# Wide attention of a fused transformer kernel: first group's key products placed ahead of its first queries, norm weights loaded ahead of the queries' weight

## The chip, the cores and the metric

The kernel runs on one core of one Trainium2 chip. The metric is the device time of one execution in microseconds (us).

## The reference

One launch computes eight residual layers on x of shape (8, 128, 512) with a context ctx of the same shape, all float32: attention, a block-sparse FFN, attention, a rotated linear layer with LoRA, the attention treated here, an fp8-quantised linear layer, an FFT-based attention, and a gated FFN with 4-bit weights. The layer that the change touches is the fifth:

```python
def _L2_xattn_ref(hidden_states, cross_attention_states, attention_mask, Wq, Wk, Wv, Wo, q_norm_w, k_norm_w):
    H, KVH, HD = (32, 8, 128)
    q = (hidden_states @ Wq.T).reshape(bsz, q_len, H, HD).transpose(0, 2, 1, 3)
    k = (cross_attention_states @ Wk.T).reshape(bsz, kv_len, KVH, HD).transpose(0, 2, 1, 3)
    v = (cross_attention_states @ Wv.T).reshape(bsz, kv_len, KVH, HD).transpose(0, 2, 1, 3)
    q = _rmsnorm(q, q_norm_w)
    k = _rmsnorm(jnp.repeat(k, GROUPS, axis=1), k_norm_w)
    scores = jnp.einsum('bhqd,bhkd->bhqk', q, k) / np.sqrt(HD) + attention_mask
    probs = jax.nn.softmax(scores, axis=-1)
    out = jnp.einsum('bhqk,bhkd->bhqd', probs, v)
    return out.transpose(0, 2, 1, 3).reshape(bsz, q_len, H * HD) @ Wo.T

x = x + _L2_xattn_ref(_layernorm(x), ctx_4096, ctx_4096, mask, Wq, Wk, Wv, Wo, q_norm_w, k_norm_w)
```

## The kernel before

The kernel is a row of stages with a barrier of all engines between two of them. The change lies in one, `wide_attention` (L1385), called once for this layer, with the settings of the class `Wide` (L1329 on). Every matrix is held as two float16 halves, high and low; a product of two matrices is three matmuls (L67 high x high, L68, L69 with a low half), so a query product of one batch is 4 x 3 matmuls of 512 columns and a key or value product is 24 matmuls of 128 columns.

The heads are worked through in 8 groups of four query heads and one key/value head, and each group in 8 batches: 64 steps of attention, numbered s = 0 to 63, and a run-in from s = -10. What each step makes is fixed by tables. Queries are made four steps ahead (`queries_at`): query 0 at s = -4, query 1 at -3, and so on. The key and value products of a group, each for two batches, follow `kv_at` (L1339): keys 0 to 3 at -4, -2, 0, 2 and values 0 to 3 at -1, 1, 3, 5, counted from the group's first step. `w_at` says when a group's weights are split into halves: the keys' weight at -10, the four quarters of the queries' weight at -9 to -6, the values' at -5, the output's four at -4 to -1.

Each engine runs its own program, written out as one loop over the same steps, strictly in program order, and waits on semaphores:

- SyncE loads the first group's weights (`load`, L1542), in between transposes the last rows of x (L1547), then the mask (L1552) and the two norm weights (L1553, L1554); in the steps it issues transposing DMAs of queries (L1562), keys (L1567) and probabilities (L1573), and the next group's weights.
- TensorE, in each step: the scores of step s, the products made at s (`make`), the mix of probabilities and values of s - 3 and the output product of s - 4. A query product needs all four quarters of the queries' weight (`weight_ready("wq", g, H - 1)`), a key product the keys' weight. All products take turns in four PSUM banks.
- ScalarE, in each step: the high half of the heads of s - 4, of value products, the squares of query and key products made at s - 1 (L1726), the high half of those made at s - 2 (L1735), the high halves of the step's weights (L1717), the exponentials (L1758). `squares` waits for the low half of the product two before of its kind, `high_of_rows` until that one's transpose has landed.
- VectorE, in each step: the low half of heads, mask and maximum (L1807, L1810), addition to x (L1826), mean of squares (L1839), low half of the probabilities of s - 1 (L1868), low half of rows made at s - 2 (L1857), the normalising of those made at s - 1 (L1844, for keys also the product with the norm weights, L1848), then the low halves of the step's weights (L1874). The two norm weights are multiplied into one at s = -4 (L1885).
- GpSimd: the root of the mean squares (L1923), the reciprocals, normalised probabilities and their high half (L1931, L1938, L1941).

The order within a step on VectorE is, in short:

```python
for use in rows_here(s):      # made at s - 1
    mean(use)
...
for use in rows_split(s):     # made at s - 2
    low_of_rows(use)
for use in rows_here(s):
    normalise(use)            # waits for the root
for use in weights_at(s):
    low_of_weight(use)
```

Of the kernel before, what the change touches and what calls it, by code (L numbers as in the profile page):

```python
# [8 lines left out]
P = 128  # L9
B = 8  # L10
# [61 lines left out]
class Kernel:  # L72
# [19 lines left out]
    def sem(self, name):  # L92
        self.in_use.append(self.nc.alloc_semaphore(name=name))
        return self.in_use[-1]
# [1234 lines left out]
class Wide:  # L1329


    def __init__(self, name, groups, dim, key_tiles, turn_at, q_ahead):
        self.name, self.groups, self.dim, self.key_tiles = name, groups, dim, key_tiles
        self.normed = name == "a2"
        self.turn_at, self.q_ahead = turn_at, q_ahead
        self.heads = 4
        self.banks = (4, 2, 1, 1)
        if self.normed:
            self.kv_at = {-4: ("k", 0), -2: ("k", 1), 0: ("k", 2), 2: ("k", 3), -1: ("v", 0), 1: ("v", 1), 3: ("v", 2), 5: ("v", 3)}  # L1339
            self.w_at = {-10: [("wk", 0)], -9: [("wq", 0)], -8: [("wq", 1)], -7: [("wq", 2)], -6: [("wq", 3)], -5: [("wv", 0)],  # L1340
                         -4: [("wo", 0)], -3: [("wo", 1)], -2: [("wo", 2)], -1: [("wo", 3)]}
        else:
            self.kv_at = {-4: ("k", 0), -3: ("k", 1), -2: ("v", 0), -1: ("v", 1), 0: ("k", 2), 1: ("k", 3), 2: ("v", 2), 3: ("v", 3)}
            self.w_at = {-9: [("wk", 0)], -8: [("wq", 0)], -7: [("wq", 1)], -6: [("wq", 2)], -5: [("wq", 3)], -4: [("wv", 0)],
                         -3: [("wo", 0)], -2: [("wo", 1)], -1: [("wo", 2)], 0: [("wo", 3)]}
        self.first = min(self.w_at)


W1 = Wide("a1", 4, 96, 2, -5, 5)
# [35 lines left out]
def wide_attention(K, A, wq, wk, wv, wo, mask=None, qw=None, kw=None, quant=None, nxt=None):  # L1385
# [12 lines left out]
    with ExitStack() as c:  # L1398
# [3 lines left out]
        sem = lambda n: K.sem(f"{N}_{n}")  # L1402
# [32 lines left out]
            return [("q", u)] if 0 <= u < TOTAL else []  # L1435

        def kv_made_at(s):
            return [(A.kv_at[s - g * B][0], g, A.kv_at[s - g * B][1]) for g in range(G) if s - g * B in A.kv_at]

        def made_at(s):  # L1440
            return queries_at(s) + kv_made_at(s)
# [28 lines left out]
        if A.normed:  # L1470
            by_row = [u for u in all_made if u[0] != "v"]
            ss_done, mean_done, root_done, row_done, row_hi, row_lo = (
                Steps(sem(n), by_row) for n in ("ss", "mean", "root", "row", "row_hi", "row_lo"))
            q_in, k_in = [sem(f"q_in{i}") for i in range(QT)], [sem(f"k_in{i}") for i in range(4)]
            col_in, col_done = sem("col_in"), sem("col_done")

        def landed(engine, use):

# [51 lines left out]
        with nc.Block() as block:  # L1530
            @block.sync
            def _(sp):
                rows = lambda w: w.rearrange("(k p) n -> p k n", p=P)

                def load(kind, g):
                    if kind == "wo":
                        src = wo[g * H * R:(g + 1) * H * R, :].rearrange("(h r) c -> r h c", r=R)
                    else:
                        w = {"wq": wq, "wk": wk, "wv": wv}[kind]
                        n = H * R if kind == "wq" else R  # L1540
                        src = rows(w)[:, :, g * n:(g + 1) * n]
                    sp.dma_start(nat[kind][:, :, :], src).then_inc(w_in[kind], 16)  # L1542

                for kind in ("wk", "wq"):
                    load(kind, 0)
                sp.wait_ge(last_lo_done, 1)
                sp.dma_start_transpose(K.xn_pair[:, :, :, LAST * P:B * P].rearrange("p a k n -> p (a k) n"),  # L1547
                                       last_hl[:, :, :].rearrange("p a n -> p (a n)")).then_inc(last_in, 16)
                for kind in ("wv", "wo"):
                    load(kind, 0)  # L1550
                if A.normed:
                    sp.dma_start(mk[:, :], mask[0, 0, :, :]).then_inc(col_in, 16)  # L1552
                    sp.dma_start(col[:, 0, :], qw.rearrange("(a d) -> a d", a=1).to_broadcast([P, D])).then_inc(col_in, 16)  # L1553
                    sp.dma_start(col[:, 1, :], kw.rearrange("(a d) -> a d", a=1).to_broadcast([P, D])).then_inc(col_in, 16)  # L1554
                for s in steps:
                    for use in rows_split(s):
                        _, _, _, src, _ = rows_of(use)
                        sp.wait_ge(row_lo.sem, row_lo.count(use))
                        if use[0] == "q":
                            if use[1] >= QT:  # L1560
                                scored(sp, use[1] - QT)
                            sp.dma_start_transpose(q_t[use[1] % QT][:, :, :, :].rearrange("p a h n -> p (a h) n"),  # L1562
                                                   src[:, :, :].rearrange("p a n -> p (a n)")).then_inc(q_in[use[1] % QT], 16)
                        else:
                            if use[1]:
                                scored(sp, s_of(use[1] - 1, 2 * use[2] + 1))
                            sp.dma_start_transpose(k_t[use[2]][:, :, :, :].rearrange("p a h n -> p (a h) n"),  # L1567
                                                   src[:, :, :].rearrange("p a n -> p (a n)")).then_inc(k_in[use[2]], 16)
                    for u in live(s - 1):
                        sp.wait_ge(plo_done.sem, plo_done.count(u))  # L1570
                        if u >= PT:
                            sp.wait_ge(o_bank.filled(u - PT), o_bank.n_filled(u - PT))
                        sp.dma_start_transpose(p_t[u % PT][:, :, :, :, :].rearrange("p a t h n -> p (a t h) n"),  # L1573
                                               p_nat[u % 2][:, :, :].rearrange("p a n -> p (a n)")).then_inc(p_in[u % PT], 16)
                    for use in weights_at(s - 1):
                        kind, g, i = use
                        if use == [u for u in all_weights if u[:2] == (kind, g)][-1] and g + 1 < G:
                            sp.wait_ge(wlo_done[kind].sem, wlo_done[kind].count(use))
                            load(kind, g + 1)
                    if s == LOAD:  # L1580
                        for last in (kv_last("k", G - 1), kv_last("v", G - 1), q_last(G - 1)):
                            sp.wait_ge(ring.filled(last), ring.n_filled(last))
                        quant.load_weight(sp, weight_in)
                        quant.load_context(sp, quant_in)
                sp.wait_ge(quant_in, 32)
# [203 lines left out]
            def _(dve):  # L1789
# [7 lines left out]
                def maxima(s):  # L1797
                    if s >= 2:
                        if A.normed:
                            dve.wait_ge(exp_done.sem, exp_done.count(s - 2))  # L1800
                        else:
                            for t in range(KTL):
                                dve.wait_ge(s_bank.freed((s - 2, t)), s_bank.n_drained((s - 2, t)))
                    for t in range(KTL):
                        dve.wait_ge(s_bank.filled((s, t)), s_bank.n_filled((s, t)))
                        if A.normed:
                            dve.tensor_tensor(masked[s % 2][:, :, :], s_bank[(s, 0)][:, :].rearrange("p (h n) -> p h n", h=H),  # L1807
                                              mk[:, :].unsqueeze(1).to_broadcast([P, H, P]), ALU.add).then_inc(s_bank.freed((s, 0)), 1)
                            dve.wait_ge(s_bank.freed((s, 0)), s_bank.n_drained((s, 0)))
                            m = dve.tensor_reduce(negmax[s % 2][:, :], masked[s % 2][:, :, :], AX.X, ALU.max, negate=True)  # L1810
                        else:
                            m = dve.tensor_reduce(negmax[s % 2][:, 2 * t:2 * t + 2],
                                                  s_bank[(s, t)][:, :].rearrange("p (h n) -> p h n", h=2),
                                                  AX.X, ALU.max, negate=True)
                    m.then_inc(max_done.sem, 1)
# [64 lines left out]
                dve.wait_ge(last_hi_done, 1)  # L1880
                dve.tensor_tensor(last_hl[:, 1, :], last_xn[:, :], last_hl[:, 0, :], ALU.subtract).then_inc(last_lo_done, 1)
                for s in steps:
                    if s == -4:
                        dve.wait_ge(col_in, 48)
                        dve.scalar_tensor_tensor(col[:, 0, :], col[:, 0, :], scale / WS, col[:, 1, :],  # L1885
                                                 ALU.mult, ALU.mult).then_inc(col_done, 1)
                        dve.wait_ge(col_done, 1)
# [1819 lines left out]
```

## Time and profile before

| what | value |
|---|---|
| median of 3 runs | 1568.62 us (1567.54 to 1570.8) |
| the profiled execution | 1571.84 us |
| its span | 1570.0 us |
| TensorE matmul busy | 1394.0 us (89%) |
| VectorE busy | 1089.5 us (69%) |
| ScalarE busy | 733.0 us (47%) |
| GpSimd busy | 728.7 us (46%) |
| mean granted clock of TensorE | 0.953 |
| stage of the change | about 697 to 1207 us of the span |

The span runs from the first to the last instruction of the profiled execution. PE is TensorE, PEld its weight loads, DVE VectorE, ACT ScalarE, POOL GpSimd, SPq the DMA issues of SyncE. A row of a timeline has the start and the duration in us, the line, the operation with output <- inputs, their shapes, and in brackets the idle time before it and what ended it. Matmuls overlap: of a run of them the distance from start to start is the price, not the duration of one. The granted clock is 1.00 at 2.4 GHz and 0.50 at 1.2 GHz.

### The profile page before, as it was taken

How to read it: one execution, taken by the hardware profiler on the slowest of the kernel's cores; microseconds unless marked ns; L12 is line 12 of the kernel's file. 1: busy time of each engine (PE TensorE's matmuls, PEld its weight loads, DVE VectorE, ACT ScalarE, POOL GpSimd, SP SyncE). 2: the span in 40 equal slices, each digit the busy share in tenths (PEclk: the TensorE clock that was granted, in tenths of full speed). 3: DMA queues.
4: the chain of work that ended last, by engine and by line, in shares of the span. 5: the costliest groups of instructions: out<-in, count | busy, mean ns of one | idle time of the engine just before them, and what ended most of it. 6: DMA issues, size and time to landing. Idle time of an engine off the chain costs nothing. (4 is left out here: it accounts for less than half of the span.)

```text
span 1570.0 us, 31373 instructions
## 1 busy us (share of the span) xinstructions
PE 1394.0 (89%) x11348; PEld 833.1 (53%) x11348; DVE 1089.5 (69%) x2159; ACT 733.0 (47%) x2388; POOL 728.7 (46%) x719
## 2 busy tenths in 40 slices
PE   5898699995999999759999999999997767659998
PEld 4775344444777777326555555555553234324444
DVE  7897565536767766757878878778778789956222
ACT  4676363212434432127666666666653356435111
POOL 4787441003434435735666666666655025744000
PEclk9999699997999999879999999999999789979999
DMA  7999571108999998556676665555445201275000
GB/s 183 181 174 169 134 155 39 23 6 172 174 181 194 157 147 145 90 111 161 120 138 111 116 131 116 112 121 100 101 78 111 97 1 38 38 151 105 14 27 28
DMA packets 524169, 174.62 MB, mean 111 GB/s; under 512 B 482560, under 2 KB 507456, under 8 KB 523888
## 3 DMA queue, kind: packets, MB, share of 16 engines
q1 hardware_dynamic: 524016, 172.62, 57.8%
q8 instruction: 92, 1.51, 0.4%
q14 instruction: 61, 0.50, 0.1%
HBM read 53.27 MB, written 2.10 MB: 35 GB/s over the span
## 5 line engine op out<-in xcount | busy, mean ns | idle before, releaser
L1923 POOL TENSOR_TENSOR a_q_ss<-a_q_ss,half 128x4 f32<-128x4 f32 x64 | 89.3, 1396 | 183.5 <-DVE a_k_ss L1839 92.8
L67 PE MATMUL bank<-a_wq_hi,xn_pair 128*128 128x512 f16 (+1 forms) x384 | 139.7, 364 | 19.7 <-DVE a_wq_lo L1874 19.0
L1758 ACT ACTIVATE a_probs<-a_masked,a_negmax 128x128 f32<-128x128 f32 x256 | 99.6, 391 | 95.3 <-DVE a_negmax L1810 95.3
L1285 POOL TENSOR_TENSOR a_p_hl<-a_probs,a_p_hl 128x512 f16<-128x512 f32 x64 | 74.3, 1161 | 143.8 <-DVE a_p_hl L1193 143.8
L69 PE MATMUL bank<-a_wq_hi,xn_pair 128*128 128x512 f16 (+1 forms) x384 | 139.5, 363 | 0.0
L68 PE MATMUL bank<-a_wq_lo,xn_pair 128*128 128x512 f16 (+1 forms) x384 | 139.4, 363 | 0.0
L67 PE MATMUL bank<-a_wo_hi,a_o_hi 128*128 128x512 f16 x256 | 98.0, 383 | 10.3 <-DVE x_state L1826 10.3
L68 PE MATMUL bank<-a_wo_lo,a_o_hi 128*128 128x512 f16 x256 | 98.0, 383 | 0.0
L69 PE MATMUL bank<-a_wo_hi,a_o_lo 128*128 128x512 f16 x256 | 97.8, 382 | 0.0
L1807 DVE TENSOR_TENSOR a_masked<-bank,a_mask 128x512 f32<-128x512 f32 x64 | 44.2, 690 | 70.0 <-PE bank L69 69.9
L1938 POOL TENSOR_TENSOR a_normal<-a_probs,a_recip 128x512 f32<-128x512 f32 x64 | 89.8, 1403 | 5.0
L716 POOL TENSOR_TENSOR a_p_hl<-a_probs,a_p_hl 128x512 f16<-128x512 f32 x64 | 77.8, 1226 | 26.3 <-DVE a_p_hl L627 15.6
L67 PE MATMUL bank<-xn_pair,f_w_t 128*128 128x512 f16 (+1 forms) x176 | 67.9, 386 | 18.8 <-DMA xn_pair<-ctx_lo 15.2
L67 PE MATMUL bank<-a_k_t,a_q_t 128*128 128x128 f16 (+1 forms) x384 | 81.1, 237 | 0.7 <-DMA a_q_t<-a_q_hl 0.7
L489 ACT ACTIVATE a_probs<-bank,a_negmax 128x128 f32<-128x128 f32 x256 | 72.7, 383 | 19.0 <-DVE a_negmax L620 18.7
L69 PE MATMUL bank<-a_k_t,a_q_t 128*128 128x128 f16 (+1 forms) x384 | 81.0, 237 | 0.0
L68 PE MATMUL bank<-a_k_t,a_q_t 128*128 128x128 f16 (+1 forms) x384 | 81.0, 237 | 0.0
L1769 ACT ACTIVATE a_o_hi<-bank 128x512 f16<-128x512 f32 x64 | 38.1, 596 | 86.2 <-PE bank L69 86.1
L1186 DVE TENSOR_REDUCE a_negmax<-bank 128x2 f32<-128x512 f32 x64 | 42.9, 691 | 50.7 <-PE bank L69 50.7
L3531 DVE SCALAR_TENSOR_TENSOR f_h<-bank,f_h 128x512 f32<-128x512 f32 (+1 forms) x22 | 15.2, 690 | 88.4 <-PE bank L69 80.1
L1127 ACT ACTIVATE a_probs<-bank,a_negmax 128x256 f32<-128x256 f32 x128 | 53.4, 472 | 37.8 <-DVE a_negmax L1186 37.8
L1726 ACT ACTIVATE a_qn<-bank 128x128 f32<-128x128 f32 x256 | 67.3, 289 | 3.7 <-PE bank L69 3.7
(441 smaller groups left out, 5016.9 us busy)
## 6 DMA issues: line engine op xcount, KB each, us to landing
a_no<-in_L_xattn_Wo SPq DMA_DIRECT2D x9, 1024.0 KB, 6.0
a_nq<-in_L_xattn_Wq SPq DMA_DIRECT2D x8, 1024.0 KB, 5.9
a_n_wq<-in_L_xattn_Wq SPq DMA_DIRECT2D x4, 768.0 KB, 6.6
a_n_wo<-in_L_xattn_Wo SPq DMA_DIRECT2D x4, 768.0 KB, 6.0
a_nk<-in_L_xattn_Wk SPq DMA_DIRECT2D x9, 256.0 KB, 3.1
a_nv<-in_L_xattn_Wv SPq DMA_DIRECT2D x9, 256.0 KB, 4.0
x_state<-in_x SPq DMA_DIRECT2D x8, 256.0 KB, 4.2
a_ctx<-in_ctx_t SPq DMA_DIRECT2D x8, 256.0 KB, 4.3
```

Of the source, the lines that this page charges most:

```text
L67: pe.matmul(out, lh, rh, start=start, stop=False)
L68: pe.matmul(out, lh, rl, start=False, stop=False)
L69: return pe.matmul(out, ll, rh, start=False, stop=stop)
L489: m = act.activation(probs[t % PS][:, h * P:(h + 1) * P], s_bank[t][:, h * P:(h + 1) * P], ACT.Exp, bias=negmax[t % 4][:, h:h + 1])
L716: pool.tensor_tensor(p_hl[t % PS][:, 1, :], probs[t % PS][:, :], p_hl[t % PS][:, 0, :], ALU.subtract).then_inc(plo_done.sem, 1)
L1127: m = act.activation(probs[u % PROBS][:, n, :], s_bank[(s, t)][:, n * KTL * P:(n + 1) * KTL * P], ACT.Exp, bias=negmax[u % 4][:, n:n + 1])
L1285: pool.tensor_tensor(p_hl[s % PN][:, 1, t, :], probs[unit(s, t) % PROBS][:, :, :].rearrange("p h n -> p (h n)"), p_hl[s % PN][:, 0, t, :], ...
L1726: m = act.activation(dst[:, h, :], src[:, h, :], ACT.Square, scale=1.0 / WS, accum_out=sums[:, h:h + 1])
L1758: m = act.activation(probs[s % 2][:, h, :], src, ACT.Exp, bias=negmax[s % 2][:, h:h + 1], accum_out=total[s % 2][:, h:h + 1])
L1807: dve.tensor_tensor(masked[s % 2][:, :, :], s_bank[(s, 0)][:, :].rearrange("p (h n) -> p h n", h=H), mk[:, :].unsqueeze(1).to_broadcast([P ...
L1923: pool.tensor_tensor(r[:, :], r[:, :], K.half[:, 0:n], ALU.pow).then_inc(root_done.sem, 1)
L1938: m = pool.tensor_tensor(normal[s % 2][:, t, :, :], probs[s % 2][:, :, t * P:(t + 1) * P], by, ALU.mult)
```

## The change

The key products of group 0 alone are made at s = -9 to -6, one a step, in place of -4, -2, 0 and 2; those of the other groups stay. The two norm weights are loaded behind the keys' weight and ahead of the queries', with a semaphore of their own, and the mask, still behind the output's weight, has another, on which VectorE waits ahead of its first use. The product of the two norm weights moves from s = -4 to s = -8.

```diff
--- before.py
+++ after.py
@@ -1344,6 +1344,10 @@
             self.w_at = {-9: [("wk", 0)], -8: [("wq", 0)], -7: [("wq", 1)], -6: [("wq", 2)], -5: [("wq", 3)], -4: [("wv", 0)],
                          -3: [("wo", 0)], -2: [("wo", 1)], -1: [("wo", 2)], 0: [("wo", 3)]}
         self.first = min(self.w_at)
+        self.first_kv_at = {**self.kv_at, **dict(zip(range(self.first + 1, self.first + 5), [("k", i) for i in range(4)]))} if self.normed else self.kv_at
+        if self.normed:
+            for s in (-4, -2, 0, 2):
+                del self.first_kv_at[s]
 
 
 W1 = Wide("a1", 4, 96, 2, -5, 5)
@@ -1435,7 +1439,8 @@
             return [("q", u)] if 0 <= u < TOTAL else []
 
         def kv_made_at(s):
-            return [(A.kv_at[s - g * B][0], g, A.kv_at[s - g * B][1]) for g in range(G) if s - g * B in A.kv_at]
+            of = lambda g: A.kv_at if g else A.first_kv_at
+            return [(of(g)[s - g * B][0], g, of(g)[s - g * B][1]) for g in range(G) if s - g * B in of(g)]
 
         def made_at(s):
             return queries_at(s) + kv_made_at(s)
@@ -1472,7 +1477,7 @@
             ss_done, mean_done, root_done, row_done, row_hi, row_lo = (
                 Steps(sem(n), by_row) for n in ("ss", "mean", "root", "row", "row_hi", "row_lo"))
             q_in, k_in = [sem(f"q_in{i}") for i in range(QT)], [sem(f"k_in{i}") for i in range(4)]
-            col_in, col_done = sem("col_in"), sem("col_done")
+            col_in, mask_in, col_done = sem("col_in"), sem("mask_in"), sem("col_done")
 
         def landed(engine, use):
 
@@ -1541,17 +1546,18 @@
                         src = rows(w)[:, :, g * n:(g + 1) * n]
                     sp.dma_start(nat[kind][:, :, :], src).then_inc(w_in[kind], 16)
 
-                for kind in ("wk", "wq"):
-                    load(kind, 0)
+                load("wk", 0)
+                if A.normed:
+                    sp.dma_start(col[:, 0, :], qw.rearrange("(a d) -> a d", a=1).to_broadcast([P, D])).then_inc(col_in, 16)
+                    sp.dma_start(col[:, 1, :], kw.rearrange("(a d) -> a d", a=1).to_broadcast([P, D])).then_inc(col_in, 16)
+                load("wq", 0)
                 sp.wait_ge(last_lo_done, 1)
                 sp.dma_start_transpose(K.xn_pair[:, :, :, LAST * P:B * P].rearrange("p a k n -> p (a k) n"),
                                        last_hl[:, :, :].rearrange("p a n -> p (a n)")).then_inc(last_in, 16)
                 for kind in ("wv", "wo"):
                     load(kind, 0)
                 if A.normed:
-                    sp.dma_start(mk[:, :], mask[0, 0, :, :]).then_inc(col_in, 16)
-                    sp.dma_start(col[:, 0, :], qw.rearrange("(a d) -> a d", a=1).to_broadcast([P, D])).then_inc(col_in, 16)
-                    sp.dma_start(col[:, 1, :], kw.rearrange("(a d) -> a d", a=1).to_broadcast([P, D])).then_inc(col_in, 16)
+                    sp.dma_start(mk[:, :], mask[0, 0, :, :]).then_inc(mask_in, 16)
                 for s in steps:
                     for use in rows_split(s):
                         _, _, _, src, _ = rows_of(use)
@@ -1804,6 +1810,8 @@
                     for t in range(KTL):
                         dve.wait_ge(s_bank.filled((s, t)), s_bank.n_filled((s, t)))
                         if A.normed:
+                            if s == 0:
+                                dve.wait_ge(mask_in, 16)
                             dve.tensor_tensor(masked[s % 2][:, :, :], s_bank[(s, 0)][:, :].rearrange("p (h n) -> p h n", h=H),
                                               mk[:, :].unsqueeze(1).to_broadcast([P, H, P]), ALU.add).then_inc(s_bank.freed((s, 0)), 1)
                             dve.wait_ge(s_bank.freed((s, 0)), s_bank.n_drained((s, 0)))
@@ -1880,8 +1888,8 @@
                 dve.wait_ge(last_hi_done, 1)
                 dve.tensor_tensor(last_hl[:, 1, :], last_xn[:, :], last_hl[:, 0, :], ALU.subtract).then_inc(last_lo_done, 1)
                 for s in steps:
-                    if s == -4:
-                        dve.wait_ge(col_in, 48)
+                    if s == A.first + 2:
+                        dve.wait_ge(col_in, 32)
                         dve.scalar_tensor_tensor(col[:, 0, :], col[:, 0, :], scale / WS, col[:, 1, :],
                                                  ALU.mult, ALU.mult).then_inc(col_done, 1)
                         dve.wait_ge(col_done, 1)
```

## Rows read from the trace of the kernel before

**Rows 1.** Busy time by stretch: start:end, length, engines' busy us (instructions), granted clock, DMA

```profile
723.80:743.70 19.90, 19.19 (x198) 13.04 (x196) 18.12 (x37) 17.26 (x84) 15.85 (x15) 1.00 0.77 154
760.00:1207.00 447.00, 441.49 (x3532) 260.56 (x3530) 358.85 (x668) 276.26 (x1235) 276.24 (x262) 1.00 0.56 108
```

**Rows 2.** TensorE's waits, 705 to 1215 us: total us, times, longest us

```profile
PE bank L67 <- DVE a_wq_lo L1874: 19.0, 1, 19.0
PE bank L67 <- DVE x_state L1826: 4.8, 4, 1.6
...
PE bank L67 <- DVE a_qn L1844: 0.7, 1, 0.7
```

**Rows 3.** Timeline of TensorE from its first matmul: start, us, line, operation, [idle before]

```profile
707.41 0.61 PE L67 MATMUL bank<-a_wq_hi,xn_pair 128*128 128x512 f16 x1 [19.03 <-DVE a_wq_lo L1874]
...
711.23 0.52 PE L67 MATMUL bank<-a_wq_hi,xn_pair 128*128 128x512 f16 x1
...
712.01 0.22 PE L67 MATMUL bank<-a_wk_hi,ctx_hi 128*128 128x128 f16 x1
...
713.35 0.38 PE L67 MATMUL bank<-a_wq_hi,xn_pair 128*128 128x512 f16 x1
```

**Rows 4.** Timeline of SyncE at the stage's start

```profile
697.62 0.50 SPq L1542 DMA_DIRECT2D a_nq<-in_L_xattn_Wq  x1
...
704.00 0.43 SPq L1553 DMA_DIRECT2D a_col<-in_L_xattn_q_norm_w  x1
704.48 0.43 SPq L1554 DMA_DIRECT2D a_col<-in_L_xattn_k_norm_w  x1
...
718.56 1.24 SPq L1562 DMA_TRANSPOSE a_q_t<-a_q_nat  x1
```

**Rows 5.** Timeline of ScalarE at the stage's start

```profile
704.20 2.19 ACT L1717 ACTIVATE a_wq_hi<-a_nq 128x512 f16<-128x512 f32 x4 [3.56 <-DMA a_nq<-in_L_xattn_Wq]
```

**Rows 6.** Timeline of VectorE at the stage's start

```profile
700.67 0.69 DVE L1874 SCALAR_TENSOR_TENSOR a_wk_lo<-a_nk,a_wk_hi 128x512 f16<-128x512 f32 x1 [0.34 <-ACT a_wk_hi L1717]
704.86 2.50 DVE L1874 SCALAR_TENSOR_TENSOR a_wq_lo<-a_nq,a_wq_hi 128x512 f16<-128x512 f32 x4 [3.49 <-ACT a_wq_hi L1717]
...
710.13 0.29 DVE L1885 SCALAR_TENSOR_TENSOR a_col<-a_col 128x128 f32<-128x128 f32 x1 [2.17 <-DMA a_col<-in_L_xattn_k_norm_w]
...
714.21 0.17 DVE L1839 TENSOR_SCALAR a_k_ss<-a_k_ss 128x2 f32<-128x2 f32 x1 [0.65 <-ACT a_kn L1726]
...
715.53 0.42 DVE L1844 TENSOR_TENSOR a_kn<-bank,a_k_ss 128x256 f32<-128x256 f32 x1
715.99 0.43 DVE L1848 TENSOR_TENSOR a_kn<-a_kn,a_col 128x256 f32<-128x256 f32 x1
```

**Rows 7.** Timeline of GpSimd: the root of key product 0

```profile
714.62 0.70 POOL L1923 TENSOR_TENSOR a_k_ss<-a_k_ss,half 128x2 f32<-128x2 f32 x1
```

**Rows 8.** Timeline of VectorE in the fill

```profile
724.95 0.68 DVE L1807 TENSOR_TENSOR a_masked<-bank,a_mask 128x512 f32<-128x512 f32 x1
...
731.81 0.69 DVE L1857 SCALAR_TENSOR_TENSOR a_q_nat<-a_qn,a_q_nat 128x512 f16<-128x512 f32 x1
```

**Rows 9.** Timeline of TensorE in the fill: scores 0 and scores 4

```profile
723.80 0.22 PE L67 MATMUL bank<-a_k_t,a_q_t 128*128 128x128 f16 x1
...
743.73 0.22 PE L67 MATMUL bank<-a_k_t,a_q_t 128*128 128x128 f16 x1
```

**Rows 10.** Timeline of TensorE in an earlier stage, around an idle time

```profile
664.57 0.58 PE L67 MATMUL bank<-f_nw,xn_pair 128*128 128x512 f16 x1 [4.60 <-PEq L2491]
...
670.50 0.41 PE L69 MATMUL bank<-f_nw,xn_pair 128*128 128x512 f16 x1
670.74 0.38 PE L67 MATMUL bank<-f_nw,xn_pair 128*128 128x512 f16 x1
```

**Rows 11.** Transposes, issue to landing in us: queries (716 to 760 us), last rows

```profile
DMA to landing us min/median/max: 3.1/3.6/4.9
...
xn_pair<-a_last_hl SPq DMA_TRANSPOSE x1, 4.8
```

## The prediction

> **What bounds the kernel now.** The change lies in one stage, the wide attention. I read first the busy time by stretch. From 760 to 1207 us TensorE is busy for 441.5 of 447 us at full granted clock [rows 1], so the body of the stage is a TensorE stream and anything that shifts this stream shifts the end. Then TensorE's waits over the whole stage: 19.0 us before its first matmul, on the low half of the queries' weight, 4.8 us near the end on the output rows, and one of 0.7 us in the fill [rows 2]. So the end of the stage is the start of the stream, plus its work, plus stalls in the fill. The TensorE timeline gives the start, 707.41. The twelve matmuls of query 0 take 4.60 us (707.41 to 711.23 for the first nine, 0.42 us from one to the next at half clock, then about 0.216; 12 x 0.216 = 2.59 is a query at full speed), and the 24 of key product 0 take 713.35 - 712.01 = 1.34 us [rows 3].
>
> **Part 1: loads.** On SyncE the two norm-weight loads, 0.43 us each, move ahead of the load of the queries' weight, which was issued at 697.62 [rows 4]. That weight is split from 704.20 [rows 5]. The two lie 0.48 us apart, so its issue slips by 2 x 0.48, about 0.9 us, and I take its landing to slip by the same, to 705.1. Two loads of 64 KB each beside 1 MB could cost a few tenths more, or less than the slip if the transfers were already queued; bounds 0.4 to 1.4. The transpose of the last rows waits for VectorE at 700.36 in both kernels. The mask keeps its place in the queue and gets a semaphore of its own; it is issued just ahead of 704.00, and its first reader runs at 724.95 [rows 8], so this costs nothing. VectorE's product of the norm weights (0.29 us, after a wait of 2.2 us [rows 6]) moves two to four steps forward. Issued at 697.6 and 698.0, the loads are 8 us ahead of that place, more than the 5.7 us from 704.48 [rows 4] to 710.13 that the second took here, so the wait goes; it was covered by TensorE's own work and returns nothing.
>
> **Part 2: the key products in front.** The keys' weight is split at 700.67 + 0.69 = 701.4 [rows 6]. TensorE, idle until 707.41 today, can run the four products from there. At half clock one takes 2.6 us (twice 1.34, less a little), so they end between 708.7 (clock up after 3.8 us, as in [rows 3]) and 711.7 (never up). Nothing waits for the third and fourth in the order below before they are there. Out of the stream, later, go 4 x 1.34 = **5.4 us**.
>
> **Part 3: what stands between.** This is the cost. ScalarE and VectorE take their work in program order, and a step's key rows stand ahead of that step's quarter of the queries' weight. Today the four quarters go through both engines back to back, 704.20 to 707.36 [rows 5, 6], and query 0 follows at once. In the changed order, VectorE must finish normalising key i (two instructions, behind a root on GpSimd) before it makes quarter i+1. One such trip, from rows: mean 0.17, root 0.70, first product 0.42, second 0.43, with handoffs of 0.05 to 0.24 [rows 6, 7], about 2.0 us; then 0.6 for the quarter. Worked forward: quarter 0 is split by 706.4 (today 704.86 + 0.69 = 705.55, plus 0.9); norm-weight product 706.6; mean of key 0 706.8; root 707.6; products 708.5; quarter 1 at 709.1; mean of key 1 709.2; root 710.0; products 710.9; quarter 2 at 711.5; mean of key 2 711.6 (its squares wait on ScalarE for the low half of key 0 at 709.6, and are done before that); root 712.4; products 713.3; quarter 3 at **713.9**. Query 0 needs all four quarters, so the stream starts at 713.9 instead of 707.4: **+6.5 us**. Three trips of 2.0 to 2.6 us and the landing give bounds of +5.2 to +8.
>
> **Part 4: the clock.** TensorE now works from 701.4 and then stands idle from about 708.7 to 713.9. A row shows what that does here: after an idle time of 4.60 us the stream at 664.57 came back at half clock (a matmul of 0.58 us where one takes 0.38 at full speed) and was at full speed only from 670.5 to 670.7 [rows 10], some 6 us later, against 3.8 us in [rows 3]. So query 0 starts slow again. Both are the same price within bounds: from -2.0 (query 0 at full speed, 12 x 0.216 = 2.6 instead of 4.6) to +1.1 (half clock for 2.1 us longer). I take **0**, as the idle time is nearest to that row's. The Trainium skill's page "TensorE: Matmul & The Clock Gate" (section "Why this matters for your kernels") says that the array must be kept busy to reach its full rate and that idle gaps between bursts throw it back; the row agrees, and by the first half of it alone, work put in front as a warm-up, the sum would be 2.0 us lower.
>
> **Part 5: the fill.** With the keys gone, TensorE from query 0 to scores 0 has four query products and one value product, 4.60 + 3 x 2.59 + 1.34 = 13.7 us, so scores 0 start at 727.6. Query 0 lands in time or nearly: today its transpose is issued at 718.56 [rows 4], behind the squares of query 1, 2.6 us after that product's end at 713.35 + 2.59 = 715.94. The same 2.6 us after 721.1 make 723.7, and 3.6 to 4.9 us to landing [rows 11] make 727.3 to 728.6. Next, scores 0 to scores 4 take 743.73 - 723.80 = 19.9 us today [rows 9]. Of these TensorE is busy for 19.19 [rows 1], with a stall ahead of query 7. Without two key products it could need 16.4. VectorE and GpSimd can't follow quite so fast: the low half of query 3 comes 731.81 - 724.95 = 6.9 us after the first masking [rows 8], behind GpSimd's normalised and cast probabilities, and this order stays. Masking begins 0.8 us after the start of scores 0, so query 3's transpose is issued 8.3 us after that start and lands 3.6 to 4.3 later, at 11.9 to 12.6; TensorE reaches scores 3 at 11.1 (three scores of 0.67, three queries of 2.59, one value product). This new stall of 0.8 to 1.5 takes the place of the old one of 0.7 [rows 2], and scores 4 start after 17.2 to 17.9. I take **+0.3** for all stalls together, bounds -0.8 to +1.
>
> **Sum:** 6.5 - 5.4 + 0 + 0.3 = **+1.4 us**. From query 8 on the order and the banks are what they were, and [rows 1] leave no slack in which the shift could vanish. The profiled execution took 1571.84 us (span 1570.0), 3.2 above the median of the runs, so its changed twin would be 1573.2; against the median, 1568.62, the forecast is **1570.0 us**.
>
> **The rivals.** *Slower, the transposes of the first keys.* ScalarE takes the high half of key 2 only when key 0's transpose has landed, and that of key 3 only after key 1's; the value weight, an output quarter and the squares of query 0 are queued behind. Key 1's transpose is issued at about 712.1; landing after 3.6 us it leaves the squares of query 0 ready at 717.1, 1.4 us before query 0 is done at 718.5. The transpose issued under the loads took 4.8 us [rows 11], still no loss. It decides from a landing of about 5 us on; at 8 us scores 0 wait 3 us more, which gives +4.4, 1573.0. For it: the loads saturate the queues early in this stage. Against it: the loads are mostly done by 710. *Near zero or slightly below, a fast clock.* TensorE keeps full speed over the gap and the scores land in time: +1.4 - 2.0 - 0.5 = -1.1, 1567.5. Against it stands the row with the 4.60 us gap. *Faster, the quarters are not held up.* If the trips fitted in front of the landing, only the 0.9 us would be lost: 0.9 - 5.4 + 0.3 = -4.2, 1564.4. The key's squares would have to run before quarter 0, and the order on ScalarE says otherwise. *The change does less than it says:* the keys leave the stream in any case, but if the four products ran no earlier than query 0 the sum would be the 0.9 us alone; the early split of their weight speaks against it, and I give it no share of its own.
>
> **How the numbers follow.** A measurement of this kernel tells about 0.2%, 3.1 us, from no change. My forecast has a chance of 0.65, its own range being -1.2 to +3.9 by the bounds of trips, clock and stalls (not all at their ends), with some 0.05 of it beyond +3.1. The late transposes have 0.17, the fast clock 0.12, the unhindered quarters 0.06. Faster by over 0.2%: 0.06. Slower by over 0.2%: 0.17 + 0.05 = 0.22. Within: 0.72. The range leaves out the unhindered quarters and the far end of the transposes: 1566.3 to 1573.8.
>
> **What would show it.** In the changed profile: key products on TensorE from about 701.4; the quarters of the queries' low weight no longer together but some 2.4 us apart, the last at about 713.9; a wait of TensorE on that weight of about 5 us instead of 19; query 0's matmuls some 0.42 us apart again; scores 0 at about 727.6, scores 4 at 744.8 to 745.5 instead of 743.73; a short wait ahead of scores 3 on the transposed query. I am wrong if the four quarters stay within 4 us, if query 0 runs at full speed from its first matmul, or if TensorE stalls beyond scores 4.

## The result and the profile after

The changed kernel takes 1576.0 us (median of five runs, 1575.38 to 1577.49), the one before beside it 1569.69 (1567.54 to 1570.8). The ratio is 1.0045 with an interval of 1.0034 to 1.0056: about 7 us slower, and 6.3 by the medians. In its profile the span is 1573.5 us.

The stage from its first load to the next stage's first load took 517.84 us (695.27 to 1213.11) against 512.23 before (697.18 to 1209.41), 5.6 us more. The stages behind it agree within 0.5 us, so the loss is in this stage. The two profiles reach the stage at different times; below, "at +x" is x us after the stage's first load (697.18 before, 695.27 after).

TensorE's waits in the stage, of the changed kernel, to be held against [rows 2]:

```profile
PE bank L67 <- DVE a_wk_lo L1882: 13.0, 1, 13.0
PE bank L67 <- DVE a_wq_lo L1882: 7.1, 1, 7.1
PE bank L67 <- DVE x_state L1834: 4.8, 4, 1.6
PE bank L67 <- DMA a_q_t<-a_q_nat: 2.4, 2, 1.4
PE bank L67 <- DVE a_o_lo L1828: 1.3, 3, 0.5
```

The wait of 19.0 us has become 13.0 and 7.1 with the key products between them; the 4.8 us near the end are as before; the wait on VectorE in the fill (0.7) is gone and 2.4 us on transposed queries have come. The marks of TensorE's stream, of the changed kernel: the first key product, query 0, scores 0, scores 3 and scores 4 (against [rows 3, 9]):

```profile
699.48 0.29 PE L67 MATMUL bank<-a_wk_hi,ctx_hi 128*128 128x128 f16 x1 [13.01 <-DVE a_wk_lo L1882]
...
714.62 0.61 PE L67 MATMUL bank<-a_wq_hi,xn_pair 128*128 128x512 f16 x1 [7.14 <-DVE a_wq_lo L1882]
...
728.35 0.23 PE L67 MATMUL bank<-a_k_t,a_q_t 128*128 128x128 f16 x1
...
741.06 0.23 PE L67 MATMUL bank<-a_k_t,a_q_t 128*128 128x128 f16 x1 [1.42 <-DMA a_q_t<-a_q_nat]
...
747.43 0.23 PE L67 MATMUL bank<-a_k_t,a_q_t 128*128 128x128 f16 x1 [0.94 <-DMA a_q_t<-a_q_nat]
```

Query 0 starts at +19.35, before at +10.23: **9.1 us later**, where 6.5 were forecast. It is again at half clock (0.61 us a matmul). Scores 4 start at +52.16, before at +46.55: 5.6 us later, and this is what the stage keeps to its end.

Where do the 9.1 us come from? SyncE's queue and ScalarE's conversions of the queries' weight, of the changed kernel:

```profile
695.27 0.38 SPq L1547 DMA_DIRECT2D a_nk<-in_L_xattn_Wk  x1
695.70 0.50 SPq L1551 DMA_DIRECT2D a_col<-in_L_xattn_q_norm_w  x1
696.25 0.43 SPq L1552 DMA_DIRECT2D a_col<-in_L_xattn_k_norm_w  x1
696.72 0.43 SPq L1547 DMA_DIRECT2D a_nq<-in_L_xattn_Wq  x1
```

```profile
705.54 0.63 ACT L1723 ACTIVATE a_wq_hi<-a_nq 128x512 f16<-128x512 f32 x1 [6.85 <-DMA a_nq<-in_L_xattn_Wq]
...
706.58 0.63 ACT L1723 ACTIVATE a_wq_hi<-a_nq 128x512 f16<-128x512 f32 x1
...
709.36 0.62 ACT L1723 ACTIVATE a_wq_hi<-a_nq 128x512 f16<-128x512 f32 x1
...
711.84 0.61 ACT L1723 ACTIVATE a_wq_hi<-a_nq 128x512 f16<-128x512 f32 x1
```

The weight is issued at +1.45 instead of +0.44, as forecast; but its first conversion starts at +10.27 instead of +7.02, **3.3 us later and not 0.9**. From that first conversion on the forecast chain is there. VectorE, of the changed kernel, with the quarters at 706.20, 708.92, 711.40 and 713.88, and one root on GpSimd:

```profile
706.20 0.69 DVE L1882 SCALAR_TENSOR_TENSOR a_wq_lo<-a_nq,a_wq_hi 128x512 f16<-128x512 f32 x1 [6.79 <-ACT a_wq_hi L1723]
...
708.92 0.68 DVE L1882 SCALAR_TENSOR_TENSOR a_wq_lo<-a_nq,a_wq_hi 128x512 f16<-128x512 f32 x1
709.52 0.16 DVE L1847 TENSOR_SCALAR a_k_ss<-a_k_ss 128x2 f32<-128x2 f32 x1
...
710.60 0.42 DVE L1852 TENSOR_TENSOR a_kn<-bank,a_k_ss 128x256 f32<-128x256 f32 x1 [0.59 <-POOL a_k_ss L1931]
711.06 0.42 DVE L1856 TENSOR_TENSOR a_kn<-a_kn,a_col 128x256 f32<-128x256 f32 x1
711.40 0.69 DVE L1882 SCALAR_TENSOR_TENSOR a_wq_lo<-a_nq,a_wq_hi 128x512 f16<-128x512 f32 x1
...
713.88 0.68 DVE L1882 SCALAR_TENSOR_TENSOR a_wq_lo<-a_nq,a_wq_hi 128x512 f16<-128x512 f32 x1
```

```profile
709.76 0.81 POOL L1931 TENSOR_TENSOR a_k_ss<-a_k_ss,half 128x2 f32<-128x2 f32 x1 [1.68 <-DVE a_k_ss L1847]
```

Between two quarters stands one trip of a key: mean 709.52, root 709.76 to 710.57, the two products 710.60 and 711.06, then the quarter 711.40: 2.48 us from quarter to quarter. From the first conversion to the last quarter it is 714.56 - 705.54 = 9.0 us, forecast 713.9 - 705.1 = 8.8. That the last quarter stands at 713.88 in the listing, as if on the forecast 713.9, is chance: this profile reached the stage 1.91 us earlier, and the forecast was for the quarter's end, at +16.7, measured at +19.3.

### The profile page after: what moved, and what is told of

Its sections match the earlier page's. It is cut to its first block and busy times, and to the rows that moved or that the text cites. A ratio compares the mean times of both kernels' runs of the same rounds, so it can differ in the third digit from the quotient of the medians.

```text
span 1573.5 us, 31374 instructions
## 1 busy us (share of the span) xinstructions
PE 1394.6 (89%) x11348; PEld 834.9 (53%) x11348; DVE 1090.8 (69%) x2159; ACT 735.6 (47%) x2388; POOL 728.2 (46%) x719
```

## The experiments

Each kernel was timed in five rounds against the kernel before on the same chip, and profiled once. T1 says that the loads in front hold up the queries' weight, T2 that it is their kind (one row read 128 times), T3 that the order of the work, and not the early products, costs the rest; R1 to R3 are their rivals. Stage lengths are worked out as above. Two profiles of before gave 512.2 and 511.2 us, two of the changed kernel 517.8 and 517.3, so differences of stages carry about 1 us; 511.7 and 517.6 are used as their values.

### loads_only: the loads alone

```diff
-        self.first_kv_at = {**self.kv_at, **dict(zip(range(self.first + 1, self.first + 5), [("k", i) for i in range(4)]))} if self.normed else self.kv_at
-        if self.normed:
-            for s in (-4, -2, 0, 2):
-                del self.first_kv_at[s]
+        self.first_kv_at = self.kv_at
```

> The changed kernel with the key products back at -4, -2, 0 and 2; the two norm-weight loads stay ahead of the queries' weight. Theory T1, the loads hold up the queries' weight behind them in the queue: the weight is split from 10.2 to 10.4 us after the stage's first load (before 7.0, changed 10.3), TensorE starts query 0 some 3.3 us later than before, at 13.5, and the kernel takes 2.7 to 3.3 us more than before. Rival R1, the weight landed late in the changed kernel because the key products or their conversions were running, and two loads alone cost the 0.9 us of their issue: split from 7.9, 0.9 us more than before.

Ratio 1.0030 (1.0017 to 1.0043), about 4.7 us; stage 517.0. ScalarE's conversions of the queries' weight, with the first load at 693.10:

```profile
703.65 2.19 ACT L1720 ACTIVATE a_wq_hi<-a_nq 128x512 f16<-128x512 f32 x4 [7.27 <-DMA a_nq<-in_L_xattn_Wq]
```

At +10.55: the landing is as late as in the changed kernel, with no early key product at all. T1 holds for the landing, R1 falls. The time is above T1's 2.7 to 3.3 us: query 0 started at +14.09, 3.9 us later than before, and the half clock lasted longer, 5.10 us for query 0 instead of 4.60 and 1.76 for key 0 instead of 1.34.

### keys_only: the early products alone

```diff
                 load("wk", 0)
+                load("wq", 0)
                 if A.normed:
...
-                load("wq", 0)
```

> The changed kernel with the queries' weight loaded ahead of the two norm weights; the key products stay in front. T1: the queries' weight is split from about 7.0 us after the stage's first load; norm weights land before quarter 0 is through VectorE or up to 1 us later; the last quarter is ready 9.0 us after the first split, query 0 starts at 16 to 17 instead of 19.35, and the kernel takes 2.3 to 3.3 us more than before instead of 6. R1: the split starts at about 10 again and the time stays at 5.5 to 6.5 us more.

Ratio 1.0015 (1.0003 to 1.0026), about 2.4 us; stage 514.4. The first conversion came at +6.4. Query 0, with the first load at 693.87:

```profile
710.05 0.57 PE L67 MATMUL bank<-a_wq_hi,xn_pair 128*128 128x512 f16 x1 [3.91 <-DVE a_wq_lo L1882]
```

At +16.2, and the part of the sum that concerned the keys alone is seen by itself: 2.7 us more than before by the stage. The norm weights, now behind the queries' weight, kept VectorE waiting for 0.6 us, until +8.36, so the first trip began that much late. T1 holds here too: the time lies in its range of 2.3 to 3.3 us, not at R1's 5.5 to 6.5.

### plain_loads and loads_only_plain: what is slow in these loads

Both take the loads as they stand in the changed kernel and in loads_only, and read the mask's 128 rows in place of one row 128 times. The norm weights are left out; the keys become zero.

```diff
-                    sp.dma_start(col[:, 0, :], qw.rearrange("(a d) -> a d", a=1).to_broadcast([P, D])).then_inc(col_in, 16)
+                    sp.dma_start(col[:, 0, :], mask[0, 0, :, :]).then_inc(col_in, 16)
...
-                    sp.dma_start(col[:, 1, :], kw.rearrange("(a d) -> a d", a=1).to_broadcast([P, D])).then_inc(col_in, 16)
+                    sp.dma_start(col[:, 1, :], mask[0, 0, :, :]).then_inc(col_in, 16)
```

> The changed kernel with both norm-weight loads, which read one row of 512 bytes 128 times, reading the 128 rows of the mask instead, of the same size (the norm weights are left out of the keys, which become zero). Theory T2, the repeated reading of one row is what is slow in the queue: the queries' weight is split 8.0 to 8.6 us after the stage's first load instead of 10.3, and the kernel takes 1.7 to 2.3 us less than the changed one, 3.5 to 4.5 more than before. Rival R2, any two loads of 64 KB in rows of 512 bytes cost this: split at 10.3, 5.5 to 6.5 us more than before.

> The kernel of loads_only (key products where they were before, two loads ahead of the queries' weight), with both loads reading the 128 rows of the mask instead of one row of norm weights 128 times (the norm weights are left out of the keys). T2, the repeated reading is slow: the queries' weight is split 7.6 to 7.9 us after the stage's first load instead of 10.55, and of the 4.7 us that loads_only cost 0.7 to 1.3 are left. R2, the place in the queue costs it whatever is read: 4 to 5 us more than before.

plain_loads: ratio 1.0019 (1.0007 to 1.0031), about 3.0 us, stage 514.9. loads_only_plain: 1.0019 (1.0008 to 1.0030), about 3.0 us, stage 513.8. Their first conversions of the queries' weight, with the first loads at 694.87 and at 694.25:

```profile
702.55 0.63 ACT L1723 ACTIVATE a_wq_hi<-a_nq 128x512 f16<-128x512 f32 x1 [4.20 <-DMA a_nq<-in_L_xattn_Wq]
```

```profile
701.66 2.19 ACT L1720 ACTIVATE a_wq_hi<-a_nq 128x512 f16<-128x512 f32 x4 [3.97 <-DMA a_nq<-in_L_xattn_Wq]
```

At +7.68 and +7.41, instead of +10.27 and +10.55. With rows of its own to read, a load of the same size and place costs 0.4 to 0.7 us against before's first profile (+7.02) and 1.1 to 1.3 against its second (+6.35), which is what I had put down for both; reading one row 128 times costs 2.6 to 3.1 us more. The landing is a little earlier than T2's 8.0 to 8.6 for plain_loads. The transfer rate (last column, GB/s; before it the busy share of the DMA engines) shows it, clearest from 3 us after the first load on. The changed kernel:

```profile
698.30:699.30 1.00, 0.00 (x0) 0.00 (x0) 0.69 (x2) 0.40 (x1) 0.00 (x0) 0.50 0.39 34
699.30:700.30 1.00, 0.82 (x8) 0.83 (x9) 0.12 (x1) 0.00 (x0) 0.00 (x0) 0.50 0.61 26
...
701.30:702.30 1.00, 1.00 (x12) 1.00 (x11) 0.00 (x0) 0.00 (x0) 0.00 (x0) 0.50 0.94 295
```

plain_loads, at the same distance from its first load:

```profile
697.90:698.90 1.00, 0.00 (x0) 0.00 (x0) 0.63 (x2) 0.45 (x1) 0.00 (x0) 0.50 0.81 198
698.90:699.90 1.00, 0.77 (x8) 0.77 (x9) 0.17 (x1) 0.00 (x0) 0.00 (x0) 0.50 0.97 364
```

and the kernel before:

```profile
700.20:701.20 1.00, 0.00 (x0) 0.00 (x0) 0.66 (x2) 0.44 (x1) 0.00 (x0) 0.50 0.96 352
701.20:702.20 1.00, 0.00 (x0) 0.00 (x0) 0.16 (x1) 0.00 (x0) 0.00 (x0) 0.50 1.05 395
```

For about two microseconds the changed kernel moves 34 and 26 GB/s where the others move 198 to 395. The trace's records of single packets show the same. In the changed kernel the 512 packets of 512 bytes of the keys' weight took 0.027 us each on average; the 256 packets of the two loads behind it, of the same size, took 0.11, the last until +7.1, and the first packet of the queries' weight started at +4.0, in plain_loads at +2.7. T2 holds for the landing and for the stages (2.7 and 3.2 us shorter); the time of plain_loads, 3.0 us more than before, is below T2's 3.5 to 4.5. The size of the loads, their place and their number are the same in both versions; only their source differs, one row read again and again or 128 rows of another tensor. By the ratios loads_only_plain kept 3.0 us of the 4.7, more than the 0.7 to 1.3 expected, while its stage was 2.1 us above before; the two measures differ by their uncertainty.

### quarters_first: the four quarters ahead of the key rows

```diff
+            at = lambda g: {**A.w_at, -9: [("wq", i) for i in range(H)], -8: [], -7: [], -6: []} if A.normed and g == 0 else A.w_at
-            return [(kind, g, i) for g in range(G) for kind, i in A.w_at.get(s - g * B, [])]
+            return [(kind, g, i) for g in range(G) for kind, i in at(g).get(s - g * B, [])]
```

> The changed kernel with all four quarters of the first group's queries' weight split at step -9, ahead of the key rows on ScalarE and VectorE. Theory T3, the chain of key rows between the quarters delays query 0 by some 6 us: query 0 starts at 13.3 to 13.8 us after the stage's first load instead of 19.35, at full clock, as the gap behind the key products is only some 1.5 us; the key rows then end at about 23 and hold up the squares of query 0, so scores 0 come 3 to 4 us earlier than in the changed kernel, not 6, and the kernel takes 2 to 3 us more than before. Rival R3, the clock and the fill set the time and the order of the quarters does not: within 1 us of the changed kernel, 5 to 7 us more than before.

Ratio 1.0035 (1.0019 to 1.0050), about 5.5 us; stage 517.0, 0.6 shorter than that of the changed kernel. The time is the rival's. The path was T3's only in its first half: query 0 started at +14.75 (forecast 13.3 to 13.8), 4.6 us earlier than in the changed kernel, and at full speed. TensorE's waits in the first 63 us of this stage, without the one ahead of the keys:

```profile
PE bank L67 <- DMA a_q_t<-a_q_nat: 5.5, 3, 3.1
PE bank L67 <- DVE a_kn L1853: 2.2, 1, 2.2
PE bank L67 <- DVE a_qn L1853: 0.7, 1, 0.7
```

It now waits 2.2 us for the PSUM bank that key 0 holds until it is normalised, 0.7 for that of a query, and 5.5 for transposed queries, whose rows stand behind the four keys' trips. The longest of these waits stands ahead of scores 0:

```profile
724.45 0.29 PE L67 MATMUL bank<-a_k_t,a_q_t 128*128 128x128 f16 x1 [3.14 <-DMA a_q_t<-a_q_nat]
```

That is +30.64, 2.4 us earlier than in the changed kernel where T3 had 3 to 4. After these 3.14 us idle TensorE was back at half clock: scores 0 and the query behind them took 4.83 us instead of 3.27, 1.6 us more. So of the 4.6 us 2.2 are lost until scores 0, 1.6 to the clock, and 0.9 are left at scores 4. What the order of the quarters took from query 0, the same trips take from its row, and the clock takes a share, as the rival had it.

### two_keys, four_keys and two_keys_late: keys behind the quarters

two_keys, against the changed kernel:

```diff
...
+        self.first_kv_at = dict(self.kv_at)
         if self.normed:
-            for s in (-4, -2, 0, 2):
+            for s in (-4, -2):
                 del self.first_kv_at[s]
+            self.first_kv_at.update({-6: ("k", 0), -5: ("k", 1)})
...
                 load("wk", 0)
+                load("wq", 0)
...
-                load("wq", 0)
...
-                    if s == A.first + 2:
+                    if s == A.first + 5:
```

four_keys, against two_keys:

```diff
-            for s in (-4, -2):
+            for s in (-4, -2, 0, 2):
...
-            self.first_kv_at.update({-6: ("k", 0), -5: ("k", 1)})
+            self.first_kv_at.update({-6: ("k", 0), -5: ("k", 1), -4: ("k", 2), -3: ("k", 3)})
```

two_keys_late, against two_keys: the two norm-weight loads go behind the output's weight, ahead of the mask.

> Of the key products of the first group only 0 and 1 are put in front, at steps -6 and -5, so that their rows come behind the last quarter of the queries' weight on ScalarE and VectorE; keys 2 and 3 stay at 0 and 2; the norm weights are loaded right behind the queries' weight and multiplied at step -5. Theory T3, the changed kernel lost by the order of the work and not by the early products themselves: query 0 starts at 10.2 to 10.5 us after the stage's first load, as before, at full clock (2.6 us instead of 4.6), scores 0 at 22 to 23.5 instead of 26.6, scores 4 some 2 to 3.5 us earlier than before, and the kernel takes 2 to 3.5 us less than before. Rival R3, VectorE and GpSimd set the pace of the fill whatever TensorE does: scores 4 within 1 us of before and the same time.

> As two_keys, with all four key products moved, to steps -6, -5, -4 and -3. T3: query 0 starts as before and at full clock; keys 2 and 3 stand between queries 0 to 2, so scores 0 come at 24.5 to 25.5; without keys in steps 0 and 2 scores 0 to 4 take some 18.5 to 19.1 us; scores 4 at 43.5 to 44.5 instead of 46.55, the kernel 2 to 3 us less than before. R3: as before.

> As two_keys, with the two norm-weight loads behind the output's weight, ahead of the mask, so near their place of before. VectorE waits for them at step -5 until about 12 us after the stage's first load. T3: query 0 starts at 10.2, at full clock, and its rows have slack, so the time is within 0.7 us of two_keys. Rival: the wait holds up the values' weight and the first query rows, scores 0 come 1 to 2 us later than in two_keys and so does the end.

Ratios: two_keys 1.0000 (0.9987 to 1.0013), four_keys 0.9999 (0.9984 to 1.0013), two_keys_late 1.0007 (0.9992 to 1.0022). Stages: 510.0, 509.0 and 513.2 us. Query 0, scores 0 and scores 4 of two_keys, with the first load at 693.65, and its waits in the fill:

```profile
703.07 0.57 PE L67 MATMUL bank<-a_wq_hi,xn_pair 128*128 128x512 f16 x1
...
715.71 0.23 PE L67 MATMUL bank<-a_k_t,a_q_t 128*128 128x128 f16 x1 [0.58 <-DMA a_q_t<-a_q_nat]
...
737.97 0.22 PE L67 MATMUL bank<-a_k_t,a_q_t 128*128 128x128 f16 x1
```

```profile
PE bank L67 <- DVE a_qn L1853: 2.7, 2, 1.9
PE bank L67 <- DMA a_q_t<-a_q_nat: 0.6, 1, 0.6
```

Query 0 starts at +9.42, straight behind the two key products. Its first matmul takes 0.57 us, the others 0.38, and the whole query 2.79 us instead of 4.60, so full speed came with its second matmul. Scores 0 come at +22.06, 4.6 us earlier than before, as T3 has it. But scores 4 come at +44.32, 2.2 earlier than in the first profile of before and 1.2 earlier than in the second: half of the gain or more is given back between the two, where TensorE waits 2.7 us for VectorE instead of 0.7, and scores 0 to 4 take 22.3 us instead of 19.9. That is R3's share. T3's gain of 2 to 3.5 us in the time is not there (ratio 1.0000); the time is what R3 had. four_keys, with the first load at 691.68, has scores 0 at +24.18 and scores 4 at +43.33, both slightly ahead of T3's forecast, and in the time again no gain (T3 had 2 to 3 us):

```profile
701.06 0.39 PE L67 MATMUL bank<-a_wq_hi,xn_pair 128*128 128x512 f16 x1
...
715.86 0.22 PE L67 MATMUL bank<-a_k_t,a_q_t 128*128 128x128 f16 x1
...
735.01 0.22 PE L67 MATMUL bank<-a_k_t,a_q_t 128*128 128x128 f16 x1
```

```profile
PE bank L67 <- DMA a_q_t<-a_q_nat: 2.4, 2, 2.0
```

two_keys_late shows what the norm weights cost when they are needed early and loaded late; VectorE, with the first load at 693.89:

```profile
707.09 0.29 DVE L1893 SCALAR_TENSOR_TENSOR a_col<-a_col 128x128 f32<-128x128 f32 x1 [3.83 <-DMA a_col<-in_L_xattn_k_norm_w]
```

It stood for 3.8 us, and scores 0 came at +25.13 instead of +22.06, behind a wait of 3.00 us:

```profile
719.02 0.29 PE L67 MATMUL bank<-a_k_t,a_q_t 128*128 128x128 f16 x1 [3.00 <-DMA a_q_t<-a_q_nat]
```

TensorE came back from it at half clock, and scores 0 with the query behind them took 6.20 us instead of 3.27. The stage is 3.2 us longer than that of two_keys, more than the rival's 1 to 2; by the ratios the difference is 1.1 us, within their intervals. So the rival holds by the stage and is not decided by the time.

### before_again, after_again, four_keys_again

These are the same kernels once more, on one chip.

> The kernel before, unchanged, as a run of its own, to see how far one profile differs from the next: the stage from its first load to the next stage's first load at 511.7 to 512.8 us (512.2 in the first profile) if the stage's length can be compared between profiles to half a microsecond; 510 to 514 if the clock's phase alone moves it by more. Ratio 1.000.

> The changed kernel once more, beside the others on one chip. The stage 517.3 to 518.4 us (517.8 in its first profile), the queries' weight split 10.0 to 10.5 us after the stage's first load, ratio 1.0035 to 1.0045. If the late landing was a chance of one execution, the split comes at 8 us and the stage is 2 us shorter.

> four_keys once more: its stage was 3.2 us shorter than the first profile of before, while the ratio of its runs to those of before was 1.000 with an interval of 0.0015. If the stage's gain is real, the stage is 508.5 to 509.5 us again and the ratio 0.998 to 0.999; if it was the phase of the clock, 510 to 512 and 1.000.

before_again: 0.9989 (0.9977 to 1.0000), stage 511.2, so a stage repeats to 1 us and not to half a microsecond. after_again: 1.0039 (1.0026 to 1.0053), stage 517.3, first conversion at +10.23: the late landing is no chance of one execution. four_keys_again: 0.9997 (0.9986 to 1.0007), stage 510.0, which is what was expected if the first gain was not real. The two stages of four_keys lie 2.2 us below those of before (509.5 against 511.7), but its time doesn't show it, and an identical copy of before came out 0.11% below it. The profiles also reach the stage at 691.7 to 699.7 us, though the instructions ahead of it are the same in all, which blurs the whole time more than the stage. So four_keys is no slower than before, clearly faster than the change, and a gain over before of some 2 us is neither shown nor excluded. I have no version that is shown to beat both.

## Why the prediction was wrong

The forecast was 1570.0 us, 1.4 over the median shown; the range, 1566.3 to 1573.8, ends 2.2 us below what was measured. The step that failed is part 1, the landing of the queries' weight behind the two small loads, priced at 0.9 us where 3.3 were measured; a second term, the stalls of the fill, was also too small. Step by step:

- **Part 1, the loads: wrong, and the largest error.** The term was a slip of 0.9 us with bounds of 0.4 to 1.4. Measured 3.3 (+7.02 to +10.27), and 3.9 between the second pair of profiles. I priced the two issues and let the bytes cost a few tenths; what the reads themselves take I put at nothing, without a row for it. The two loads read one row 128 times, and against loads with rows of their own this cost 2.6 to 3.1 us more. The trace of before may have held a sign of it: the second of these loads took 5.7 us from issue to use, behind loads of a megabyte, and I used the figure only for when their product could run. None of the rivals had a late landing of this weight in it.
- **Part 2, early products: right.** They ran from +4.2 (699.48) to +12.2, with the clock up on the way, and nothing waited for the third or fourth.
- **Part 3, the trips: right.** 9.0 us from first conversion to last quarter, forecast 8.8; the quarters 2.72, 2.48 and 2.48 us apart, forecast 2.7, 2.4 and 2.4. With the landing as measured the forecast's own chain gives a start 8.9 us later, measured 9.1.
- **Part 4, the clock: right.** After 7.14 us idle, where 5.2 were forecast, query 0 came back at half clock and took 4.43 us. From query 0 to scores 0 it took 13.73 us, forecast 13.7. The warm-up shows only where there is no gap or a short one: in two_keys and four_keys, and in quarters_first after 2.25 us idle. After 3.91 us, in keys_only, query 0 was at half clock again.
- **Part 5, the fill: too small.** +0.3 was taken. With the start 9.1 later and 5.4 out of the stream, scores 4 at 5.6 later leave 5.6 - 9.1 + 5.4 = 1.9 us for stalls (1.8 in the second pair), beyond the bound of +1. VectorE and the transposes, in the changed kernel:

```profile
728.16 0.69 DVE L1852 TENSOR_TENSOR a_qn<-bank,a_q_ss 128x512 f32<-128x512 f32 x1 [0.90 <-POOL a_q_ss L1931]
...
730.22 0.68 DVE L1815 TENSOR_TENSOR a_masked<-bank,a_mask 128x512 f32<-128x512 f32 x1
...
736.96 0.69 DVE L1865 SCALAR_TENSOR_TENSOR a_q_nat<-a_qn,a_q_nat 128x512 f16<-128x512 f32 x1
...
741.68 0.68 DVE L1865 SCALAR_TENSOR_TENSOR a_q_nat<-a_qn,a_q_nat 128x512 f16<-128x512 f32 x1
```

I had masking start 0.8 us after scores 0; it started at 730.22, 1.9 after 728.35, as VectorE was still at query 2, whose root it had waited for, and then at two quarters of weights. The 0.8 was too short for the rows of before already: there it is 1.15 us (724.95 after 723.80). The low half of query 3 follows at 736.96, and scores 3 at 741.06, 12.7 after scores 0 where I had 11.9 to 12.6. The wait of 1.42 us ahead of them was forecast at 0.8 to 1.5. The low half of query 4, at 741.68, was issued at 742.39 and landed at 747.4, 5.0 us later, where I had allowed 4.3 though [rows 11] go up to 4.9. This second wait, 0.9 us, was not in the sum at all. No run changes VectorE's order or the transposes alone, so this part is read from the trace and not tested.

The sum with measured terms is 9.1 - 5.4 + 0 + 1.9 = 5.6 us, the length by which the stage grew. Against the forecast of 1.4 that is 4.2 us more: 2.4 from the landing, 0.2 from the trips and 1.6 from the stalls. By these figures either large error alone would have left the time inside the range. The two parts of the change are not simply additive: the loads alone cost 5.3 by the stage (4.7 by the ratio), the keys alone 2.7 (2.4), together 5.9, 2.1 us less than the sum of both. One reason is the clock: in loads_only the half clock cost query 0 and key 0 0.9 us more than before (5.10 and 1.76 us for them instead of 4.60 and 1.34), in the changed kernel it did not. Most of the rest lies ahead of query 0: against the mean of the two profiles of before it starts 4.2 us later with the loads alone and 6.3 with the keys alone, in the changed kernel 9.4, about 1 less than the sum; 0.6 of this is the wait for the norm weights that keys_only alone has. My rival of late transposes named the right kind of cause, a queue that is slow to deliver, but the wrong transfer: ScalarE began the squares of query 0 at 719.25, as the product ended, so the first keys' transposes cost nothing. The last rows' transpose took 9.5 us instead of 4.8 and nobody waited for it.

## What to carry to other kernels

Before a small load is moved in front of a large one that the start of a stage waits for, look at what it reads: a row spread over all partitions can hold up what is behind it far longer than its bytes say, here by 2.6 to 3.1 us for two loads of 64 KB. Work put into idle time of one engine brings rows that the others must handle in program order; put it behind what the first big product needs. Here that took back the loss, but no gain over the kernel before is shown. And once TensorE is relieved in a fill, find which engine limits next before counting the relief as gain.

## What the hardware showed that I had not expected

Two loads of 64 KB, each reading one row of 512 bytes 128 times, kept the queue at 26 to 34 GB/s for about 2 us, where loads of 128 separate rows in the same place left 198 to 364. What in the path of the reads is slow was not measured. SyncE itself was held up too: the issue of the transpose behind these loads took 2.28 us instead of 1.25, that of the output's weight 1.90 instead of 0.54, and with rows of their own (plain_loads) the two took 1.24 and 0.68.
